# Another interleaving of the 42 chains of steps in a two-layer sequence kernel

## What is computed

```python
x = x + linear_attention(layernorm(x))   # 16 heads of 8, state decays by a token's own factor
x = x + moe0(layernorm(x))               # top 2 of 8 experts, 352 wide
x = x + ssm(layernorm(x))                # conv of 3, then a selective scan with 16 states
x = x + moe1(layernorm(x))               # top 2 of 8 experts, 128 wide, and 2 shared ones
```

## Time and profile before

| | us |
|---|---|
| median of 3 runs | 1800.45 |
| lowest, highest | 1800.25, 1806.42 |
| span of the profiled execution | 1833.6 |
| busy in it: PE, DVE, ACT, POOL | 1401.7, 1361.4, 981.4, 929.9 |

### The profile page before, as it was taken

The page is one execution under the profiler, slowest core; times in us unless marked ns, Lnnn a source line. Parts: engine busy times, 40 slices in busy tenths (PEclk is TensorE's granted clock), DMA queues, the critical chain, the costliest instruction groups (busy, mean ns, idle before and its releaser), DMA issues.

```text
span 1833.6 us, 29178 instructions
## 1 busy us (share of the span) xinstructions
PE 1401.7 (76%) x9192; PEld 943.1 (51%) x9192; DVE 1361.4 (74%) x2543; ACT 981.4 (54%) x1663; POOL 929.9 (51%) x571
## 2 busy tenths in 40 slices
PE   6674899988999789688578567787836776767668
PEld 3342577755776556555355434565613553435345
DVE  6793969788997889649586588288759579639836
ACT  2213262638756666378264554677446575477332
POOL 1000422385451856828838588400278737852875
PEclk9886899999999999989889579889969788879879
DMA  9995373757884669858477678888468767876952
GB/s 238 162 184 116 90 208 119 212 137 249 281 263 137 215 218 292 230 145 281 148 213 169 185 231 220 231 291 281 125 200 247 200 202 250 225 209 210 287 111 50
DMA packets 320067, 369.53 MB, mean 202 GB/s; under 512 B 33801, under 2 KB 260521, under 8 KB 319657
## 3 DMA queue, kind: packets, MB, share of 16 engines
q1 hardware_dynamic: 277672, 336.05, 62.8%
q0 software_dynamic: 42240, 31.61, 9.6%
HBM read 306.09 MB, written 63.42 MB: 202 GB/s over the span
## 4 chain that ended last, share of the span: by engine, by line
PE 23%; issue 16%; POOL 16%; DVE 15%; ACT 11%; SPq 9%; DMA 7%; another core or an unknown queue 1%; POOLq 0%; DVEq 0%; ACTq 0%
POOL x L886 7%; POOL rows_D L867 5%; PE bank L991 3%; DVE arena_c L1516 3%; POOL rows_B L867 2%; PE bank L1063 2%; SPq L664 2%; SPq L686 2%; DVE arena_c L1502 2%; DMA x<-outs,slot_idx 2%; DMA arena_c<-bc_rows 2%; DVE arena_c L1511 2%; PE bank L1098 2%; DVE arena_a L1443 1%; PE bank L951 1%
## 5 line engine op out<-in xcount | busy, mean ns | idle before, releaser
L886 POOL DMA_INDIRECT x<-outs,slot_idx x240 | 465.4, 1939 | 205.2 <-issue 110.7
L991 PE MATMUL bank<-arena_c,ident 128*128 128x512 f32 x512 | 289.2, 702 | 96.9 <-DVE arena_c L1502 95.9
L1516 DVE TENSOR_TENSOR_SCAN arena_c<-arena_c 128x1024 f32<-128x1024 f32 x128 | 292.1, 2283 | 1.8
L909 PE MATMUL bank<-xT_ring,mix 128*128 128x128 f16 (+1 forms) x1296 | 240.9, 225 | 58.0 <-DVE mix L1688 16.7
L910 PE MATMUL bank<-xT_ring,mix 128*128 128x128 f16 (+1 forms) x1296 | 240.4, 225 | 0.0
L911 PE MATMUL bank<-xT_ring,mix 128*128 128x128 f16 (+1 forms) x1296 | 240.3, 225 | 0.0
L1063 PE MATMUL bank<-mix 128*128 128x128 f32 (+1 forms) x1296 | 192.2, 295 | 60.4 <-ACT yrow L1319 36.2
L1063 PEld LDWEIGHTS bank<-mix 128*128 128x128 f32 (+1 forms) x1296 | 172.9, 205 | 96.0 <-issue 86.0
L991 PEld LDWEIGHTS bank<-arena_c,ident 128*128 128x128 f32 x512 | 104.9, 222 | 218.9 <-DVE arena_c L1502 121.7
L867 POOL DMA_INDIRECT rows_D<-xrow,slot_idx x112 | 187.7, 1676 | 40.1 <-issue 30.1
L867 POOL DMA_INDIRECT rows_B<-xrow,slot_idx x128 | 182.2, 1423 | 46.0 <-issue 35.0
(11 more groups left out here) (225 smaller groups left out, 2460.4 us busy)
## 6 DMA issues: line engine op xcount, KB each, us to landing
arena_c<-bc_rows SPq DMA_DIRECT2D x256, 512.0 KB
mix<-weights_B SPq DMA_DIRECT2D x168, 352.0 KB
mix<-weights_B SPq DMA_DIRECT2D x168, 192.0 KB
outs<-yrow SPq DMA_DIRECT2D x156, 128.0 KB
mix<-weights_D SPq DMA_DIRECT2D x144, 128.0 KB
xg<-rows_B SPq DMA_DIRECT2D x84, 129.0 KB
xg<-rows_D SPq DMA_DIRECT2D x72, 129.0 KB
mix<-weights_D SPq DMA_DIRECT2D x144, 64.0 KB
```

Source lines behind the costliest of these rows:

```text
L886: pool.indirect_dma_start(out=x[:, b, j, :], out_offset=None, in_=y_d[q], in_offset=bass.IndirectOffsetOnAxis(ap=slot_idx[:, q % RJ, c, i ...
L909: pe.matmul(o, hi, xh, start=True, stop=False)
L991: last = pe.matmul(bank[C_BANKS[h]][:], ident[:], half(hb[:, n % RR, :], h), start=(n == 0), stop=(n == NS - 1))
L1516: dve.tensor_tensor_scan(hb[:, n % RR, :], dA[:, n % RDA, :], hb[:, n % RR, :], 0.0, ALU.mult, ALU.add).then_inc(c_scan.sem, 1)
```

## The change

`ORDER` is replaced by another string of the same 4917 letters, 52 lines of the source. Each chain still gives its steps in its own sequence, and no instruction, buffer or wait of a step is changed; what changes is which chain's turn it is. The first two lines of both:

```diff
@@ -72,52 +72,52 @@
             self.wait_empty(w, before)
 
 ORDER = (
-    "AAAAAAAAAPAAAAWAAAAAAAAAAAAWAAAoWAsokqAswokqAswokqAswokqAswokqAswokqAswokqAswokqAswoCwAqswoqAswoqAswoqAswoqA"
-    "swoqAswCqCAwCAoAsWqWwWAwAPAAAAPWAWAAAAAAAPWWAAAAAAAAAWWoWWAsWokqAswokqAswokqAswokqAswokqAswokqAswokqAswokqAs"
...
+    "AAAAACAAAAAAAAAAPAAACAAAAAACAAAAoAoAsqkossqAoAoAwsoAqksokwqkAwsosAqwokqksqwwAoqAwskoAskwsqwoqqwAwsoAswoAqwqw"
+    "ossAoAqAqwwsqwAAAwAAAAWAAWAAAAWAAAAAAAWAAAWAoWAsWoAqoAsWWowqwAWsksqkCosAqqkowWPkAkswPwoqsAWokkAoAsWwPqqkwosq"
...
```

More of the change, by code:

```diff
@@ new lines @@
+    "VMVwwAZPANTKPAULKeUZULReAVULMVRUwUTMLAPAPANKATAPVSUZLAAVNUUKPMeAAVLARVZPULUAUeLAAASPANAKVVATAAPAZAUoSLUUVASs"
+    "MKNoLAVsqXoPULRUTUZAPwRqKLskMkoqAVPTwULVoskAXXUXsMVwoPRXAqUqoskwPAwLkKVsoUSUkLAeTqUwsSoqskeAKNoMwKALqZVXskeX"
+    "VowUANXPLwZsoqUAqPPoVwUARsSPqoRwPKsTqwMAUoLswTVAoNUqPwqsAZqsqLUAPeMALwPVSwwUSAPRwNLVTKPUZAUMeLeAVPAPUNAPLRVP"
+    "PUUTZPLNMAPVPKPSZUPPPeLPSVAUKSeAPUPARLAAVRPKANATVAAMeUGAZNGAASZPALURRGPAUTLGAMeVAANZTGMUoVAsoKTLUqUAVNLVwkos"
+    "ZGsMeNUAkRKqLqoUULkRATsZwVoUVMAUkLUwLKsoRKATVqqGVoswAksoqGkXwsUUMLqSUAkkwTLVVoCUUALosSeUXeKNMACCCSweqwoALsVS"
@@ new lines @@
+    "CoCqCsCXUZLAVRqoCKXCqUAXCsCCsCCoCsUCAXCCoCACCXTCKCCNCoSAwXVwLqCsVMZewAAXRCSqsUUNCwbwqwZxdwqbccdqLTxwUwMhwVLA"
+    "UXpVdhbXXXNdXxAZeKyAApcAbXPAAUecAhAAbLpxNAVASAXhdAUAAAAAAAZPPPpeAASPbosAKoSdPLxPPyNhRAVTRMUPUxcoLbkRhpecPUPy"
+    "bVKPLcTMVTxULqAUbUBZpMcsPLsdVNdPRdUhVZoPeyykLxkUUKATxyMpqNRLZKqdVUoAbVUThspeohLwSSUMsRNkVwUZAqwTLLsqVUcKoNqw"
+    "kkRpAbyZeVUxSMULLRwcsNoVTsxZAhUyqpoVdAUGhcKdMsbypqewUoedkdNwbLVTGZsLxhUSKwVcAoqNZekUxAMywoUGqRLALVcKdRGysUpo"
+    "UTwNwhAbMqsSVUosKeLwLAVUqRbxUeoVLhSwdTKZyAqsMUsRVTAwULMNZSoqUcGVLwpTMVNUbUsSAZqLGxeyULKApwqRcVwhANAwyATAKVRU"
@@ new lines @@
+    "PMLUAxpPAcUhAZALyTAPARAVVUKeSpMULPTAyUSMeVLCCGAPCUPVPKSPCNGCPPeCPPZSUPLCPULPVPAVUCRACCUPCCCTLCAMKCPCCUACCCCA"
+    "CCCACANKPCCCACCCPSAZPAXNoeAsVoCLUAVCCoSRXZsPeLbsNAUVbqXodPkcxkUTLMseZAXUwXqVohLUUdXANKxXLXPXbXXkVpcPwPRVXSoX"
+    "xXXSZkbsqhAduowxeRldTdXvcKbhANqZpyeuNsylqvSMUpTRcULUboZLwnxhAMVpywcVbTUdUhKpLxyqkUsnhckaeVcbqxdpMwLoNZKeRSPU"
+    "VUsbLUVhkAoTNLMVpsAyZxURqRocskxUsqPTLAUyKNowwdMLdSVURbcZPdLTshVAMeyohKUUVLPwAbqNPpTeoSwAPywUqVUZpKsoNPSxLceh"
+    "MPdSVRUAcpxGULyVPqhyTUSZbLUNVMLZGsKUobxVpeUGdRyqLUhVLVcebdTMKRxAwNbxdupAlRZvuBhNwlUwvxcZqhLTUpnUsKGVswMdncUL"
@@ new lines @@
+    "dqyyVAbhpLxUGaeTcqwpKyUGNRGcSRMwVyhLUVpUAeLyCUZLSCTMGNCVwKZVCUTUCLeURCLNMKTMCVSVAZSUAeUCLKUCRLNAVCPZCUVRUeTC"
+    "LKUVCSLACPPMRKNUPLTVMUSUZLTVBCCVSMPSUCPCPLUCRUPCPTMGKCACPPPCCLPeVCVSKPUPUCCLPeUCCPCNCAKCAZAVGCAGeRLNAZCUALeA"
+    "PNVdPAPTAUAXUAdVMUbbxXLxLRdVXScZUAhULhKpTbVNxdAMUAcVRAPbLUehZTbAxPUXpMKAcSdcSVNoZyAeUxLbshpVLyPoXANZchSoepyX"
+    "qdbXsUUsAXoXSpVLVuNlxvukScylZewxhAdbvkqcRshbuxXoNZlXRypdnAKcPXXXbvosuXpPSyhKlnTXMUwkvycqdxakqpALbcPnyqhowUxS"
+    "TPVGUdenMAdhPRPPbpUPewLPsPVaNoxPLcURpKdsURGwkskATKoLMGVTxqyVZhUNMGhcAUpLkdbGZepkwbKoTqMySVNRUeScwLxAdxqRTKwh"
@@ new lines @@
+    "ZMdVbsweeRcyoTKsbUqqepLyNZKVhNxGMpRdcKsAcTLMUZSVRNLhyGoVSxeGqsZywThpUwAMpKLNeKGUoZVLTGyyAGCsNVqKCRwMqUCReZGS"
+    "TSMwoNTReUACLKKCeMCGZCGTVoLesNGUwZMVCAqCUKsSRoLKqsCwwCLCqCVTwMwCCCSCPCUCPRCLeVPSCTNMeCKZGDCPCKUeRCPGCCPPNCCV"
+    "GZCGeNCPKPLPPPeCSCPSPZVPKeRCNSPdcZdcTGMbSePNTURMULVbLPPZKTVMNRSKBZTRUxSxGSNXMZhLRXVpTUeMeLbhbXXRVUdyxXTpXNLd"
+    "dcMZSPhNKTUVbxcZLSpbyhxNScMXUpZhVPPNXycxLXdVpXXPZXXXhbPyXNdpdyPxbulxdhZvycnSpcXbSyhxudSlbpvdychxecnbbdphypdc"
+    "xahcPPbPxPphRdRPbcpyuKxlTvuMnlRdGThvxdUpMGnTPLcbURbyULhVpUccLyayGMGxVyTKGxUhhNRppUGePZyyKLCVCVCCCGUGMLUTUCCV"
@@ L121 @@
+    "ULSELENZEVNEVuZlSNRvEKZGSuElTGMvNULeGZEnEGRVuElnTKavNuSMeZlnUvLnVFIaNJFZIEJOQFISOJFIQJOFOQIJFQIJSFIJSOFOQIJS"
+    "FIJQFIGOOJQFIQOOJFQIJFQOIQJFIOJOQFOGIJQFQIOJQGOGQGQGGGGGG"
 )
```

61 lines of the change are left out of this document (17 added, 44 removed).

## The result

The changed kernel takes 1825.65 us (median of 4 runs, 1818.9 to 1834.65); the kernel before, run again beside it, 1803.18 us (4 runs, 1800.25 to 1806.42). The ratio is 1.0116 with a 95% interval of 1.0077 to 1.0155: slower by 14 to 28 us, where the prediction had no change. The time lies inside the stated range (1774 to 1827), near its upper end, but the likeliest case, the sum's 1800, was wrong.

A forecast was written before the change was run, and what follows sets the result against it. The kernel was taken as bound by handovers, not by an engine; 24 - 17 + 4.5 - 3.5 - 6 - 3.7 + 1.5 = -0.2 us on the profiled 1833.6, less 33.1 carried over, gave about 1800 us, range 1774 to 1827.

The forecast's parts named there:

- the sum: Likeliest case, all parts added: -0.2 us on the profiled span, about 1800 us; chance 0.34.
- Part 1: Start: the wait for set C, now ahead of batch 0's work, makes the first `m_lo` +24.6 us later; 24 taken.
- part 5: Everything else in the order, a mean shift of 3 places on PE and DVE: costed at nothing, 10 us either side.
- wait for the kept weights: DVE's 22.06 us idle before batch 0's first `m_lo` would go, if the kept weights are in time: -22.1.
- Part 2: Batch 2's SSM norm: its 1/sqrt no longer stands behind all of job 2's gathers; -17 us, bounds -10 and -20.
- Part 3: Job 5's `m_lo`: the 23 us stall stays, but now stands ahead of five short DVE steps; +4.5 us.
- part 4: More 1/sqrt: batch 3 -3.5, batch 7 -6, dense batch -3.7; batch 1 and A norms between +1.5 us.
- R1: Rival: the start costs its full wait, +35 to +40 in place of 24, giving 1813 us; chance 0.17.
- R2: Rival: some of the start's 24 us come back behind, leaving +8, thus 1784 us; chance 0.18.
- R3: Rival: POOL becomes the bound between 917 and 1000, slow gathers +9 and scatters +3, giving 1812 us; chance 0.11.
- The clock's 4 us: PE's restart after idling to 55 us runs below full speed: +4, kept for the range; chance 0.04.
- The carry-over from the span: Whole kernel: the 33.1 us by which the runs' median 1800.45 lies below the profiled span 1833.6 were carried over.

The follow-up runs named there:

- e1: The kernel before, unchanged, run and profiled once more: ratio 1.0003 to the kernel before, median 1808.82 us.
- e3: The kernel before with only the steps up to batch 0's first `m_lo` in the changed order: ratio 1.0199, median 1840.37 us.
- e5: The kernel before with only the wait for set C moved early, to sixth place: ratio 1.0031, median 1821.74 us.
- e10: e5 with peaks, scale, splits and keeps at the changed places, slices in the old order: ratio 1.0156 to the kernel before.
- e2: The changed kernel with all steps up to batch 0's first `m_lo` in the order of before: ratio 0.9889 to the kernel before, median 1788.57 us.
- e4: The kernel before with only job 2's second batch of 16 gathers moved behind batch 2's 1/sqrt, two more and the bias: ratio 0.989, median 1787.48 us.
- e7: e2 with the last ten gathers of job 2 moved back ahead of job 4's scatters: ratio 0.988 to the kernel before.
- e6: The changed kernel with the wait for set C and two conv steps back among batch 0's slices: ratio 0.99 to the kernel before, median 1797.06 us.

## Why the prediction was wrong

**Part 1 with part 5's "nothing" was the step that failed: the size of the start's loss.** The mechanism was the forecast one: set C landed when it did, PE and DVE began at 53 to 56 us, the waits of 7 us and 19 us went. The sum said +24.6. Against e1, the first `m_lo` came 37.4 us later in e3 and 32.0 and 32.5 later in the two profiles of the changed kernel. The place itself, forecast for 185, was at 188.2 and 188.7; the forecast was that near only because it counted from 160.9, where e1 has 156.15. Term by term, from e1 and e3, with the peaks, steps and slices from e5, e10 and e3:

| term | predicted | measured |
|---|---|---|
| start of PE's first transposes | +44.2 | +45.7 (56.1 - 10.4) |
| wait for set C among the slices | -6.3 | -7.3 |
| wait for the kept weights | -22.1 | -18.9 |
| peaks, now on the path | +6.2 | +6.9 |
| three more steps ahead of `m_lo` | +2.6 | +3.0 |
| DVE's waits for PE's products, slices reordered | 0 | +9 |

These add up to 38.4. Two terms carry most of the miss of 13 us, the slices' 9 and 3 of the kept weights. The slices' order was put into part 5, "I cost it at nothing", although this is the one stretch where DVE has no slack once it starts late: e5 has it busy for 98.18 of 107.5 us. And the wait for the kept weights was read from one execution, in which set B landed 4.7 us later than in the second; a place that is paced by transfers is not the same place in every execution, and a credit taken from it is uncertain by as much.

**Part 2, the gathers, was right,** at the far end of its bounds: -17 predicted, -21 in e2 at `shift_C` of batch 2 (750.8 against 771.7), and -21 for e4 as a whole. The fear that the weight stream would be late next was unfounded. POOL's idle time before the scatters took the moved gathers.

**Parts 3 to 5 behind the start came within 8 us by luck.** The sum had -7.2 for them beside the gathers (+4.5 - 3.5 - 6 - 3.7 + 1.5); e2 and e4, with and without them, are equal (0.9889 and 0.989), so together they gave nothing. The places show larger terms that cancel, of other signs and sizes than the sum's (start in us):

| place | e1 | e4 | e2 |
|---|---|---|---|
| job 5's first `m_lo` (its wait) | 900.6 (17.7) | 877.6 (10.2) | 873.4 (6.1) |
| batch 3's `shift_C` | 966.7 | 944.4 | 956.8 |
| last shift, dense batch | 1737.5 | 1710.4 | 1714.0 |
| from it to the dense softmax (L1561) | 11.3 | 12.6 | 27.3 |
| from it to the end of the span | 70.7 | 73.0 | 77.6 |

Part 3 said that the stall before job 5's `m_lo` stays. In the changed order it was 2.14 to 6.09 us in four profiles (and no wait in e7), in the nine of the old order 10.24 to 24.75. Behind it, batch 3's norm lost most of that again. And part 5 put the end at nothing. In the plan, the dense batch's choice of experts now has 70 steps from its shift (`d_shift`) to its end (`d_choose`), where it had 23. DVE's timeline of e2:

```profile
1713.95 0.17 DVE L1408 SCALAR_TENSOR_TENSOR arena_a<-arena_a 128x8 f32<-128x8 f32 x1 [10.48 <-POOL arena_a L840]
...
1741.27 0.21 DVE L1561 TENSOR_REDUCE arena_a<-arena_a 128x8 f32<-128x64 f32 x1
```

So the 3.7 us of the earlier 1/sqrt in part 4 were gained and more than lost: the tail is 7 us longer in e2 and in the changed kernel (78.0) than in e1. That the steps in between are the cause is likely, but no run put that one piece of order back.

**The rivals.** R1's loss of 35 to 40 us for the start is the size that was measured, but its 1813 is only 13 above the 1800 it starts from, where +21 came, and its mechanism is not the right one: the kept weights were in time, and nothing was late but DVE's own work and PE's products for it. R2, absorption further on, is refuted by e3, where 31 of 37 us are left at the end. R3's slow gathers are there (10.14 us), but their place in the order does not matter (e7). The clock's 4 us were put at the wrong place: the restart ran at full speed, and half speed came some 17 us later (0.52 in e3's 72 to 86 us), in the slices.

**The carry-over from the span.** 33.1 us were carried from the profiled span to the runs. e1's span of 1808.2 beside a median of 1808.82 shows that the two agree, and that the first profile was of a long execution.

## What to carry to other kernels

A wait that is moved ahead of the work it doesn't guard costs the time until its event, less the slack that was there anyway, and that slack can be spent only once: here the reordered slices and late peaks by themselves fitted into it (e6 lost nothing), the wait by itself used it up (e5 was 17 us later at the first `m_lo`), and together they were 37 us later. Before costing "the rest of the order" at nothing, ask whether the stretch still has idle time after the big term is in. And a small instruction that stands behind a train of transfers on an in-order queue, with three engines waiting for it, is worth a look: moving 16 gathers behind one 1/sqrt gave 1.1%. A forecast that adds up may do so by cancelling terms: compare places in the trace, and not only the sum.
